# Output sum of p and gated q made by TensorE matmuls into one PSUM block, with input loads issued ahead of the stores

## What is computed

```
# layer 0: v = group_norm(x);  A = softmax(v^T v) over channels (256 x 256)
x = x + gamma * (v A) + v
# layer 1: h = group_norm(x) scaled to 0..1 by its smallest and largest value
measures = box sums of h over 2x2, 4x4, 8x8, 16x16 pixels
alphas, sim = a fit of log(measures) against log(scale), pixel by pixel
excite = sigmoid(relu(mean(alphas) w1 + b1) w2 + b2)          # one gate per image and channel
x = x + sim * sigmoid(batch_norm(alphas)) + (1 - sim) * (h * excite)
```

## Time and profile before

| | |
|---|---|
| Time of three runs | 6600.68, 6618.52, 6620.09 us (median 6618.52) |
| Profiled execution | 6632.39 us, span 6630.7 us |
| PE busy | 5047.4 us (76%), weight loads 4635.9 us (70%) |
| DVE busy | 5429.1 us (82%) |
| ACT busy | 4779.8 us (72%) |
| POOL busy | 1760.3 us (27%) |
| Mean granted TensorE clock | 0.909 of full speed |

### The profile page before, as it was taken

One profiled execution on the slowest core, in us unless ns is written; L12 is line 12 of the kernel. 1 busy time (PEld: TensorE's weight loads), 2 busy tenths in 40 slices (PEclk: granted clock), 3 DMA queues, 4 the chain that ended last, 5 costly groups with the idle time before them and its releaser, 6 DMA issues.

```text
span 6630.7 us, 108223 instructions
## 1 busy us (share of the span) xinstructions
PE 5047.4 (76%) x35320; PEld 4635.9 (70%) x35320; DVE 5429.1 (82%) x6453; ACT 4779.8 (72%) x5203; POOL 1760.3 (27%) x1201
## 2 busy tenths in 40 slices
PE   6968887688858888588867888588876877466643
PEld 5757776688848888578857888588866777466642
DVE  1349998699968999699987999699997999599961
ACT  0118887588858888488866888488876888588851
POOL 0022222422233222322214222322214222333310
PEclk9989999899979999799989999799988999788865
DMA  3635554577756777477756777477765666455556
GB/s 115 196 123 169 177 176 150 163 241 245 246 166 204 248 248 241 134 250 249 248 181 195 249 251 242 134 240 251 247 196 176 220 222 223 131 187 180 183 184 228
DMA packets 874519, 1344.72 MB, mean 203 GB/s; under 512 B 38704, under 2 KB 694096, under 8 KB 857936
## 3 DMA queue, kind: packets, MB, share of 16 engines
q1 hardware_dynamic: 837456, 1208.16, 53.2%
q0 software_dynamic: 36864, 134.23, 10.7%
HBM read 671.16 MB, written 536.87 MB: 182 GB/s over the span
## 4 chain that ended last, share of the span: by engine, by line
PE 31%; ACT 18%; DMA 17%; issue 16%; DVE 14%; POOL 3%; SPq 1%; DVEq 0%; ACTq 0%; POOLq 0%
PE even L530 12%; DMA xa<-in_x_dram 7%; DMA x1t<-logs 6%; PE h_ps L511 5%; PE g_ps L488 4%; ACT logs L706 3%; PE odd L530 2%; PE even L532 2%; ACT logs L735 2%; DMA hr<-h_scratch 2%; DVE ut L1013 2%; DMA qd<-q_scratch 2%; PE g_ps L489 2%; ACT logs L722 2%; ACT odd L706 2%
## 5 line engine op out<-in xcount | busy, mean ns | idle before, releaser
L530 PE MATMUL even<-band,t 128*128 128x128 f32 x12288 | 1891.2, 286 | 470.5 <-ACT logs L706 313.2
L530 PEld LDWEIGHTS even<-band,t 128*128 128x128 f32 x12288 | 1660.9, 201 | 525.0 <-issue 448.9
L387 POOL TENSOR_TENSOR t<-t 128x1024 f32<-128x1024 f32 (+3 forms) x800 | 1339.6, 1686 | 1157.6 <-DVE logs L997 1114.6
L706 ACT ACTIVATE logs<-even,col 128x1024 f32<-128x1024 f32 x512 | 571.0, 1115 | 945.5 <-PE even L530 944.8
L511 PE MATMUL h_ps<-mix,xt 128*128 128x256 f32 x4096 | 994.2, 386 | 183.3 <-ACT xt L693 182.6
L428 POOL DMA_DIRECT2D x1t<-logs x256 | 226.4, 884 | 2933.4 <-DVE ut L1013 2863.6
L511 PEld LDWEIGHTS h_ps<-mix,xt 128*128 128x128 f32 x4096 | 737.5, 190 | 313.6 <-ACT xt L693 233.3
L488 PE MATMUL g_ps<-xa 128*128 128x257 f32 x2048 | 652.5, 401 | 259.5 <-DMA xa<-in_x_dram 259.4
L532 PE MATMUL even<-band,t 128*128 128x128 f32 x4096 | 791.9, 275 | 0.0
L892 DVE CUSTOM_DVE_ANT_0 h_out<-h_ps,shift,mx 128x512 f32<-128x512 f32 x512 | 382.9, 748 | 361.3 <-PE h_ps L511 356.7
L532 PEld LDWEIGHTS even<-band,t 128*128 128x128 f32 x4096 | 621.9, 192 | 0.0
(11 more groups left out here) (184 smaller groups left out, 10311.4 us busy)
## 6 DMA issues: line engine op xcount, KB each, us to landing
xa<-in_x_dram SPq DMA_DIRECT2D x256, 512.0 KB, 4.6
xb<-in_x_dram SPq DMA_DIRECT2D x256, 512.0 KB, 5.5
h_scratch<-h_out SPq DMA_DIRECT2D x128, 1024.0 KB, 7.0
hr<-h_scratch SPq DMA_DIRECT2D x256, 512.0 KB, 6.4
q_scratch<-ut SPq DMA_DIRECT2D x256, 512.0 KB, 2.7
x1t<-logs POOLq DMA_DIRECT2D x256, 512.0 KB, 5.1
p_scratch<-x1t SPq DMA_DIRECT2D x256, 512.0 KB, 3.1
pd<-p_scratch SPq DMA_DIRECT2D x256, 512.0 KB, 6.0
```

Of the source, the lines that this page charges most:

```text
L387: ins = g.tensor_tensor(dst[:, hf, d:d + n, :], src[:, hf, d:d + n, :], src[:, hf, e:e + n, :], ALU.add)
L530: ins = t.matmul(o, src[:, hf, at, :], band[:, which, :], start=True, stop=(which < 3))
L706: a.activation(dst, src[:, :], ACT.Ln, bias=col[:, EPSR:EPSR + 1]).then_inc(log_ready[which], 1)
```

## The change

DVE's sum is removed. For each of the 8 pixel blocks of a unit PE now runs two ordinary matmuls into the same 128 columns of `o_ps`: the p block as the stationary operand against the identity, which starts the group, and the q block against a diagonal matrix of the gates, which is added to it. The second operand `gates` (128 x 2 x 128) is made by two small DVE operations at the end of each turn's serial stretch, as the identity times NE. PE waits for `gate_ready` at the start of each turn that has a phase D, and for `pq_loaded` instead of DVE's `sum_ready` in each unit. On SP, the loads of A, B and D move into a function `loads` and are called one unit earlier, after the h and output stores and ahead of `store_pq`; the loads of a turn's first unit come before the turn's loop, behind the wait for the last p and q stores, which earlier stood before the p load alone.

```diff
             def turn_back(unit, n, hf, d):
                 if d == 0:
-                    pe.wait_ge(sum_ready, unit + 1)
+                    pe.wait_ge(pq_loaded[hf], 32 * (n + 1))
                 pe.wait_ge(o_copied, 2 * unit + d + 1)
                 for r in range(4):
-                    ins = t.transpose(o_ps[:, r * CH:(r + 1) * CH], pd[:, hf, (4 * d + r) * W:(4 * d + r + 1) * W],
-                                      ident[:, :])
+                    o, at = o_ps[:, r * CH:(r + 1) * CH], slice((4 * d + r) * W, (4 * d + r + 1) * W)
+                    t.matmul(o, pd[:, hf, at], ident[:, :], start=True, stop=False)
+                    ins = t.matmul(o, qd[:, hf, at], gates[:, hf, :], start=False, stop=True)
                 ins.then_inc(o_filled, 1)
...
             def turn(s, A, Bs, Cs, Ds):
                 image_of[0] = s - 2
+                if Ds:
+                    pe.wait_ge(gate_ready, s - 2)
...
-            def p_plus_q(n, unit, hf):
-                dve.wait_ge(pq_loaded[hf], 32 * (n + 1))
-                d.scalar_tensor_tensor(pd[:, hf, :], qd[:, hf, :], cols(NE)[:, hf:hf + 1], pd[:, hf, :],
-                                       ALU.mult, ALU.add).then_inc(sum_ready, 1)
...
                 d.tensor_scalar(cols(NE), cols(NE), col[:, INVP:INVP + 1], -1.0, ALU.mult, ALU.mult).then_inc(dve_done, own.one())
                 dve.wait_ge(dve_done, own.now())
+                if not (isinstance(b, int) and b == 0):
+                    dve.wait_ge(o_filled, 64 * b + 2)
+                d.tensor_scalar(gates[:, 0, :], ident[:, :], cols(NE)[:, 0:1], None, ALU.mult).then_inc(dve_done, own.one())
+                dve.wait_ge(dve_done, own.now())
+                d.tensor_scalar(gates[:, 1, :], ident[:, :], cols(NE)[:, 1:2], None, ALU.mult).then_inc(gate_ready, 1)
...
# SP, per unit: behind the h and output stores
+                if hf == 0:
+                    loads(s, i, k, 1, A, Bs, Ds)
+                elif k == 0:
+                    loads(s, i, 1, 0, A, Bs, Ds)
+                elif not last:
+                    loads(s, i + 1, 0, 0, A, Bs, Ds)
                 if Cs and not began:
                     store_pq(u - 2, nC - 1, hf)
```

More of the change, by code:

```diff
@@ L47 @@
 ACT_PAIR, ACT_IMAGE = 24, 196
-DVE_MIN_PAIR, DVE_PAIR, DVE_IMAGE = 4, 32, 374
+DVE_MIN_PAIR, DVE_PAIR, DVE_IMAGE = 4, 32, 375
 class Count:
@@ L148, in mk_conv_preact @@
         mx = sb("mx", [128, 4])
+        gates = sb("gates", [128, 2, 128])
         mins = sb("mins", [128, 2 * CHUNKS])
@@ L189, in mk_conv_preact @@
         pq_loaded = [sem("pq_loaded0"), sem("pq_loaded1")]
-        sum_ready = sem("sum_ready")
+        gate_ready = sem("gate_ready")
         o_filled = sem("o_filled")
@@ L252, in store_pq, with loads @@
                 sp.dma_start(p_dram[unit], x1t[:, hf, :]).then_inc(pq_stored[hf], 16)
-            def half_chunk(s, i, k, hf, A, Bs, Cs, Ds, first, last):
+            def loads(s, i, k, hf, A, Bs, Ds):
                 n = 16 * s + 2 * i + k
-                nb, nC, nd = n - 16, n - 32, n - 48
-                u, ud = 2 * nC + hf, 2 * nd + hf
-                began = first and k == 0
+                nb, nd = n - 16, n - 48
+                ud = 2 * nd + hf
                 if A:
@@ L268, in half_chunk @@
                 if Ds:
[L269 to L272, removed]
                     sp.wait_ge(o_filled, 2 * ud)
@@ L276, in half_chunk @@
                     sp.dma_start(qd[:, hf, :], q_dram[ud]).then_inc(pq_loaded[hf], 16)
+            def half_chunk(s, i, k, hf, A, Bs, Cs, Ds, first, last):
+                n = 16 * s + 2 * i + k
+                nb, nC, nd = n - 16, n - 32, n - 48
+                u = 2 * nC + hf
+                began = first and k == 0
                 if Cs and not (began and hf == 0) and not (last and (k, hf) != (0, 0)):
@@ L308, in turn @@
                             load_rows(first + m, 1 - m, hf)
+                if Ds:
+                    for p in pq_stored:
+                        sp.wait_ge(p, 32 * CHUNKS * (s - 2))
+                        apart()
+                loads(s, 0, 0, 0, A, Bs, Ds)
                 def pair(i, first, last):
@@ L540, in turn_h, with turn_back @@
                 ins.then_inc(odd_filled, 1)
-            def turn_back(unit, hf, d):
+            def turn_back(unit, n, hf, d):
                 if d == 0:
-                    pe.wait_ge(sum_ready, unit + 1)
+                    pe.wait_ge(pq_loaded[hf], 32 * (n + 1))
                 pe.wait_ge(o_copied, 2 * unit + d + 1)
                 for r in range(4):
-                    ins = t.transpose(o_ps[:, r * CH:(r + 1) * CH], pd[:, hf, (4 * d + r) * W:(4 * d + r + 1) * W],
-                                      ident[:, :])
+                    o, at = o_ps[:, r * CH:(r + 1) * CH], slice((4 * d + r) * W, (4 * d + r + 1) * W)
+                    t.matmul(o, pd[:, hf, at], ident[:, :], start=True, stop=False)
+                    ins = t.matmul(o, qd[:, hf, at], gates[:, hf, :], start=False, stop=True)
                 ins.then_inc(o_filled, 1)
@@ L572, in half_chunk @@
                 if Ds:
-                    turn_back(2 * nd + hf, hf, 0)
+                    turn_back(2 * nd + hf, nd, hf, 0)
                 if A:
@@ L578, in half_chunk @@
                 if Ds:
-                    turn_back(2 * nd + hf, hf, 1)
+                    turn_back(2 * nd + hf, nd, hf, 1)
             image_of = [None]
@@ L1022, in half_chunk @@
                     two = two_squares(v, vf)
-                if Ds:
-                    p_plus_q(nd, 2 * nd + hf, hf)
                 if tail:
```

## The result

The changed kernel took 6696.02 us (median of 4 runs, 6691.83 to 6700.67) against 6619.31 us before (median of 4 runs, 6600.68 to 6631.02), a ratio of 1.0119 with a 95% interval of 1.0094 to 1.0143. The profiled execution took 6694.37 us with a span of 6692.6 us.

The account below looks back on a forecast made before the run. ACT's loop of 20.23 us a unit, stretched by late input, bounds full turns; PE would become the bound. +53 - 39 - 23 + 12 + 24 = +27 us, forecast 6646 us, 0.4% slower; whole range 6592 to 6725.

Parts of the forecast that it names:

- PE becomes the bound of full turns: Turns 3 to 7: PE's loop grows from 19.52 to 21.45 us a unit, above ACT's 20.23; full turns +53 us.
- The gap at `mix_x`: Full turns: PE's 0.67 us gap, waiting for ACT's copy, goes, leaving 0.68 of the first `turn_back`'s 1.35 us.
- the wait for the log: Full turns: PE's wait for the first log remains, since PE's own box sum starts that log.
- The input wait: PE's wait for late `xa` goes with loads issued about 20 us before use; 34.5 us a full turn could be lifted.
- Rival 5: Loads ahead arrive late and input waits add to PE's loop, or matmuls cost over two instructions: 6850 us and above; chance 0.05.
- DVE's saving: DVE saves one operation of 1.29 us per half unit, but in full turns DVE does not set the period.
- Turn 2: Moved loads and no new matmul: period from 20.80 to 19.5 us, -39 us (bounds 0 and -42).
- Starts of the turns: First unit of each full turn runs at PE's pace, some 2 us longer: +10 us over five turns.
- Turn 8: No gram rows, so PE stays under ACT's 20.23; with PE's gaps filled, period 20.3 us: -23 us.
- Turn 9: Second half block's chain is hidden at full clock, late at half; lower clock in fewer units: +12 us (bounds -5 and +43).
- Turn 10: Chunk 13.2 us at 2.4 GHz, 17.7 at 1.2; mostly full clock expected: +24 us over 16 chunks (bounds -5 and +69).
- Rival 1: The clock pays: TensorE keeps 2.4 GHz through turns 9 and 10, -5 us each, about 6600 us; chance 0.12.

Follow-up runs that it names:

- the last experiment's kernel: Changed kernel with twelve matmuls that nothing reads added per unit, in turn 9 alone, ahead of the second half block: 6684.93 us, ratio 1.0099.

## Where the prediction was right, and where it was off

- PE becomes the bound of full turns: right, and in size. 21.45 us a unit was forecast, 21.43 measured. The price, 0.112 us an instruction and two for a matmul, stands in L564 and L565; the factor of 2 against transposes stands as well, not 4. The gap at `mix_x` went, and the wait for the log stayed at 0.86.
- The input wait goes: right, but the reason was incomplete. The matmuls alone remove it in full turns. Rival 5, input waits on top, is refuted from both sides.
- DVE's saving is worth nothing in full turns: right for the changed kernel, where PE sets the period. In the loads-only kernel, where PE does not, leaving the sum out was worth 13 us of the full turns' 3128. The prediction's "641 us of work in 32 units" is too low: DVE is busy 610 to 611 us in the 30 units between the marks, 20.4 us a unit.
- "The waits that SP now has ahead of it are older units' and already met": right for the loads, but what was moved behind them was not asked about. The later p store holds ACT up, which PE's longer loop hides in full turns of this kernel and turn 8 pays.
- Turn 2: -39 forecast, -42 measured.
- Starts of the turns: +10 forecast; behind turns 3 to 7 +17 measured, and +3 behind turn 2. In turn 5, PE's first unit went from 20.66 us before (2744.43 to 2765.09) to 25.22 (2719.08 to 2744.30). The two half blocks are 2.7 of the 4.6, since nothing there absorbs them, and the second box sum ran at 1.2 GHz, 3.76 us in place of 2.04:

```profile
2724.23 3.76 PE L545 MATMUL even<-band,t 128*128 128x128 f32 x16 [0.52 <-POOL t L402]
```

  I had taken PE's 2 us of a steady unit. The lower clock at that place is chance: it was there at the start of all five full turns of this trace, but the last experiment's kernel, which is the same up to turn 8, has it in one of five. The stretches behind turns 3 to 7 are 5 us shorter in all there. Turn 5 there:

```profile
2720.59 2.03 PE L545 MATMUL even<-band,t 128*128 128x128 f32 x16 [0.52 <-POOL t L402]
```

  No wait on the `gates` operations shows among those of PE.
- Turn 8: -23 forecast, -12 measured. Filling PE's gaps reduced the falls of the clock from 15 to 3. The step was right for the matmuls, which alone gave 20.23 us a unit and no fall; what it left out is ACT's wait for the p store under the new SP order, 13 us.
- Turn 9: +12 forecast, +27 measured. The chain of the second half block, transposes and box sum is late at 1.2 GHz, as the step said; only I had the lower clock go from more units. It fell in all 30, for a shorter time (clock 0.91 against 0.86 before between the same marks), and the longer half block made each fall count.
- Turn 10: +24 forecast, +27 measured, with the clock at 0.86 in place of 0.50. A chunk took 13.7 to 14.0 us at full clock and 15.9 to 17.5 where the clock fell in it; 13.2 and, at 1.2 GHz throughout, 17.7 had been worked out. The 13.2 does not follow from the step's own terms (four times 1.35 on, twice 1.29 off), so the +24 was chosen between bounds of which the lower was wrong, and that it came so near is partly luck. Rival 1 (the clock pays) has its decision point there: over 0.9 in turn 10 and 0.95 in turn 9 were wanted, 0.86 and 0.91 granted. By the rule on idle gaps that the prediction took from the Trainium skill (TensorE: Matmul & The Clock Gate, HAM oscillation), the denser turn 10 would rise to full clock, which it did for most of the time (0.86), but not at nearly no cost.
- The sum was +27 and the medians moved by 77. The traces moved by 62; the 35 between that and the forecast are +15 in turn 9, +11 in turn 8, +7 and +3 at the starts of turns, +3 in turn 10 and -3 and -1 in turns 2 and 3 to 7. The other 15 us is that the profiled execution of before was 13 us above its median. Its runs lie 30 us apart, and the longer ones have the lower granted clock (0.914 in a run of 6596.76 us, 0.908 in one of 6636.52). How much of that was in the full turns' 21.16 no run separates.

What stays open: what loads ahead would give with a p store that is not held up, and how much of the 20.55 us of the loads-only units without a fall, over ACT's 20.23, is that store and how much DVE. The traces price neither by itself, and no run moved the one or, with PE's wait filled, removed the other.

## What to carry to other kernels

Before work is moved from the busiest engine, find the loop that sets the period: here DVE had the highest busy share and its operation was worth next to nothing, while 2.7 us on PE turned a gain of 75 us (loads ahead alone) into a loss of 77. Two edits in one change need their own runs: one paid and one cost more. Where transfers are moved ahead in an ordered list, look also at what now stands behind them and at who waits for that. Count instructions, not calls: an ordinary float32 matmul in place of a transpose is two for one. Where a transposed block only has to be added to, transpose one operand and add the other's product onto it.

## What the runs showed that I had not expected

TensorE's clock is a price of slack. In full turns it fell 28 times with the loads alone, 13 and 7 times with 16 and 24 instructions a unit for the output, and not once with 32; each fall made PE the late engine for a unit, and each came behind a wait of ACT for the p store, which the new order had brought. Four useless matmuls a unit took 50 us off the loads-only kernel (0.9885 to 0.9816 of the kernel before, intervals apart). The changed kernel, with PE full, had no fall in any full turn between its marks and ran 150 units within 21.33 to 21.66 us. Its runs also spread over 9 us, where those of before spread over 30.
